# Regrouping the attention stage's PSUM products, its per-engine order and the code bias in a fused embed, attention and ranked-FFN kernel

## The reference, cut to what matters

```
h = h + attn(layernorm(h))      # 12 heads of 64; softmax over the 93 tokens of a sequence
h = h + ffn(layernorm(h))

attn: w = x @ w_qkv
      norm2 = sum over tokens of w*w                  # one per head and channel
      logits = sum over channels of w*w/norm2, * temp
      Pi = softmax(logits);  Pi_norm = Pi / (sum(Pi) + 1e-8)
      dots = sum over tokens of Pi_norm * w*w
      out = -(w * Pi) / (1 + dots);  return out @ w_out + b_out
ffn:  z = x @ P;  scores = z . C                      # 8 groups of 64 keys, 16 wide
      top 4 scores of each group -> softmax -> w
      h = gelu(z @ W1[top] + b1);  y = h @ W2[top] + b2
      code = sum over the four of y*w
      return gelu(code @ G1 + g1b) @ G2 + g2b
```

## Time and profile before

| what | us |
|---|---|
| median of 2 runs (1399.41 and 1400.19) | 1399.8 |
| the profiled execution | 1400.24 |
| its span, first to last instruction | 1398.2 |

### The profile page before, as it was taken

One profiled execution on the slowest core, in us unless ns is written; L12 is line 12 of the kernel. 1 busy time (PEld: TensorE's weight loads), 2 busy tenths in 40 slices (PEclk: granted clock), 3 DMA queues, 4 the chain that ended last, 5 costly groups with the idle time before them and its releaser, 6 DMA issues.

```text
span 1398.2 us, 34230 instructions
## 1 busy us (share of the span) xinstructions
PE 1236.3 (88%) x12232; PEld 622.2 (44%) x12232; DVE 1099.5 (79%) x3359; ACT 1093.8 (78%) x2708; POOL 1007.3 (72%) x724
## 2 busy tenths in 40 slices
PE   3943799999999999858999999999999999999995
PEld 3932466666666666623333333333333333333332
DVE  5682488888888888857878888888888888888883
ACT  0244467776777777339999999999999999999994
POOL 7731467657765776527798888888898888879884
PEclk8966899999999999869999999999999999999997
DMA  9564312222222231133313323232413322241410
GB/s 280 160 126 74 56 53 77 67 70 84 85 68 68 75 97 54 51 107 91 71 38 82 74 61 64 56 75 52 96 48 86 65 57 64 57 92 42 89 38 11
DMA packets 95704, 107.05 MB, mean 77 GB/s; under 512 B 12772, under 2 KB 92668, under 8 KB 95254
## 3 DMA queue, kind: packets, MB, share of 16 engines
q1 hardware_dynamic: 91184, 96.00, 26.6%
q10 hardware_dynamic: 2240, 5.08, 2.2%
q0 software_dynamic: 2112, 3.79, 1.0%
HBM read 67.88 MB, written 33.71 MB: 73 GB/s over the span
## 4 chain that ended last, share of the span: by engine, by line
ACT 28%; PE 11%; POOL 7%; DVE 4%; issue 4%; SPq 1%; DMA 0%; POOLq 0%; DVEq 0%; ACTq 0%
ACT ring L1076 18%; ACT arena L1088 9%; POOL arena L828 5%; PE code L1749 5%; PE ring L1736 5%; DVE arena L1484 4%; PE ring L1768 2%; POOL arena L836 1%; POOL arena L834 1%; ACT arena L1084 0%; DMA bias_codes<-arena 0%; ACT arena L1096 0%; SPq L618 0%; PE ring L1759 0%; SPq L623 0%
## 5 line engine op out<-in xcount | busy, mean ns | idle before, releaser
L1484 DVE TENSOR_TENSOR arena<-ring,arena 128x496 f32<-128x496 f32 x1008 | 611.5, 668 | 132.9 <-ACT ring L1076 129.1
L828 POOL TENSOR_TENSOR arena<-arena 128x992 f32<-128x992 f32 x264 | 608.2, 2316 | 114.1 <-ACT arena L1088 103.1
L1076 ACT ACTIVATE ring<-ring 128x496 f32<-128x496 f32 x1008 | 543.8, 689 | 12.0 <-PE ring L1736 11.1
L1736 PE MATMUL ring<-arena,w_stack 99*32 99x496 bf16 x6144 | 428.3, 375 | 25.9 <-DVE arena L1484 20.0
L1749 PE MATMUL code<-arena,w_pad 128*32 128x496 f32 x3072 | 389.0, 580 | 3.7 <-ACT arena L1092 3.3
L1736 PEld LDWEIGHTS ring<-arena,w_stack 99*32 99x32 bf16 x6144 | 159.7, 95 | 414.9 <-DVE arena L1484 253.1
L1088 ACT ACTIVATE arena<-ring 128x992 f32<-128x992 f32 x252 | 282.7, 1122 | 3.5 <-POOL arena L828 2.8
L1578 PE MATMUL ring<-arena 96*128 96x372 f32 x384 | 135.3, 489 | 1.4 <-ACT arena L932 0.9
L1749 PEld LDWEIGHTS code<-arena,w_pad 128*32 128x32 f32 x3072 | 96.6, 110 | 53.4 <-DVE arena L1484 17.8
L764 POOL TENSOR_TENSOR arena<-arena 128x372 f32<-128x372 f32 x96 | 91.9, 986 | 34.5 <-DVE arena L1324 34.5
L1627 PE MATMUL ring<-arena 128*128 128x376 f32 x192 | 78.5, 534 | 24.2 <-DVE arena L1319 16.0
(11 more groups left out here) (144 smaller groups left out, 1434.8 us busy)
## 6 DMA issues: line engine op xcount, KB each, us to landing
arena<-gates SPq DMA_DIRECT2D x48, 496.0 KB, 6.7
gates<-arena SPq DMA_DIRECT2D x16, 744.0 KB, 11.5
arena<-h_scratch SPq DMA_DIRECT2D x32, 279.0 KB
arena<-z_parts SPq DMA_DIRECT2D x144, 62.0 KB, 2.7
h_scratch<-arena SPq DMA_DIRECT2D x16, 279.0 KB
z_parts<-arena SPq DMA_DIRECT2D x48, 93.0 KB, 2.1
arena<-h_scratch SPq DMA_DIRECT2D x12, 372.0 KB
out_h<-arena SPq DMA_DIRECT2D x12, 372.0 KB
```

The source lines that it names most:

```text
L828: p_.tensor_tensor(spaces[quad % SPACES][:, j:j + 2], hid[:, POOL_DUOS.index(duo) % 2], gst[:, block // EB, j:j + 2], ALU.mult).then_inc(s ...
L1076: a_.activation(product, product, ACT.Gelu_apprx_tanh).then_inc(s_hid, 1)
L1484: v_.tensor_tensor(spaces[quad % SPACES][:, j + p], duo_bank(duo, p), gst[:, block // EB, j + p], ALU.mult).then_inc(s_gat, 1)
L1736: mm = t_.matmul(bank[32 * q:32 * q + 32], w1s[:, x + 32 * q:x + 32 * q + 32], zst[:, o, j + p], start=True, stop=True)
```

## The change: what it does

- `spread_pi` and `scores` become four products each on 32 rows of the contraction, one to a bank: `spread_pi` from `pix`, a tile [128, 94] that needs no placing, so `pi_placed`, `pis`, `unitsel` and `pi_scale_placed` go. Five of the six spreads lie side by side in each bank, and `w_pi` waits for the first five together.
- PSUM is shared out anew: `w_product` has banks 0 to 3, spreads and scores too; logits, bias and scales move to bank 6, z to the code bank.
- `head_weights` becomes one instruction. `mean_term` moves from DVE to POOL, as a negation and a product.
- `pass_sp` loads x first; bias and scales are stored a pass later.
- All five orders are rewritten, with one more pass on SP, ACT and PE.
- Stage 3: ACT's `copy_code` goes, DVE adds the bias straight from PSUM after duo 7, POOL only scales. ACT's table for gelu is loaded after the last `top4_exp`.

```diff
 def pass_sp(i):
-    store_codes(u3), store_bias(u3), store_scales(u3), load_x0(n2), store_h1(u1), load_xr(n1), store_gates(u2)
+    load_x0(n2), store_bias(u4), store_scales(u4), store_gates(u3), store_codes(u2), store_h1(u1), load_xr(n1)
...
+p_.tensor_scalar_mul(nm[k], mv[k][:, :, 0], -1.0)             # in POOL's rstd
+def mean_term(k, u): ... p_.tensor_tensor(nb[k], nm[k], rs[k], ALU.mult)
 def pass_pool(i):
+    attended(u1, 2..5), z_rest(u2), shift(u2, 0), shift(u2, 1), z_part3(u2), rstd("A", n2), residual_biased(u0),
+    rstd("G", u1), mean_term("G", u1), w2_pi(u0, 0), mean_term("A", n2), w2_pi(u0, 1..5), shift(u2, 2), attended(u0, 0..1)
...
 def pass_act(i):
+    w_copy(u1, 3..5), z_copy(u3), z_part1(u3), top4_exp(u4), scores_copy(u3, 0..1), z_part2(u3), scores_exp(u3, 0),
+    scores_copy(u3, 2), logits_exp(u1), gates_copy(u4, 2), scores_exp(u3, 1), gates_copy(u3, 0..1), copy_bias(u4),
+    norm("G", u2), copy_xT("A", u0), norm("A", n1), w_copy(u0, 0), copy_scales(u4), w_copy(u0, 1), copy_xT("G", u2),
+    scores_exp(u3, 2), w_copy(u0, 2)
...
 def pass_dve(i):
+    dots_scaled(u1), bn_stats_x0(n2), dots_negated(u1), top4(u3, 2), neg_attn(u1), mark(u3, 2), norms_floored(u0),
+    norms_inverted(u0), top4_shifted(u3), head_weights(u0), raw(u3, 2), top4_summed(u3), bn_aggr("A", n2),
+    scales_made(u3), top8(u2, 0), logits_tempered(u0), top8(u2, 1), top4(u2, 0), logits_max(u0), mark(u2, 0),
+    pi_recip(u0), top4(u2, 1), pi_made(u0), raw(u2, 0), pi_sum(u0), mark(u2, 1), pi_sum_eps(u0), residual(u1, 0),
+    pi_complete(u0), raw(u2, 1), residual(u1, 1), bn_stats_h1(u1), bn_aggr("G", u1), w_pi(u0, 0..4), attn_dots(u0, 0),
+    w_pi(u0, 5), attn_dots(u0, 1..3), top8(u2, 2), attn_dots(u0, 4..5)
...
 def w_product(u, c):
-    if c < 2: wait(pe, s_rsc, CH * (u - 1) + 5 + c)
-    else: wait(pe, s_wsq, CH * u + c - 1)
+    if c == 0: wait(pe, s_rsc, CH * u)
+    if c >= 4: wait(pe, s_wsq, CH * u + c - 3)
...
 def scores(u, s):
-    wait(pe, s_sc, SUB * u + s)
-    t_.matmul(banks[2][0:ST, :], zf[:, ST * s:ST * s + ST], cbd, ...)
+    if s == 0: wait(pe, s_wsq, min(CH * (u + 3), CH * UNITS)); wait(pe, s_rsc, min(CH * (u + 2), CH * UNITS))
+    for j in range(PAIRS):
+        rows = slice(32 * j, 32 * j + 32)
+        last = t_.matmul(ring[0:ST, j, 128 * s:128 * s + 128], zf[rows, ST * s:ST * s + ST], cbd[rows, 128 * j:128 * j + 128], ...)
...
 def spread_pi(u, c):
-    t_.matmul(pair0[:, c % 2, 0:UB * (N + 1)], headsel[:, c], pis.rearrange("p b n -> p (b n)"), ...)
+    if c == 0: pe.wait_ge(s_wsq, CH * (u + 1)); wait(pe, s_sc, SUB * (u - 1))
+    if c == 5: pe.wait_ge(s_rsc, CH * u + 5)
+    x = (N + 1) * (c % 5)
+    for b in range(UB):
+        rows = slice(32 * b, 32 * b + 32)
+        last = t_.matmul(ring[:, b, x:x + N + 1], headsel[rows, c], pix[rows], ...)
...
 def pass_pe(i):
+    out_product(u2, 2), gates_transposed(u3, 0), spread_pi(u1, 0..4), bias(u4), gates_transposed(u3, 1),
+    scales_transposed(u4), transposes("A", u0), spread_pi(u1, 5), w_product(u0, 0..1), transposes("G", u2),
+    w_product(u0, 2..5), z_product(u2), scores(u2, 0..2), logits(u0), out_product(u1, 0), gates_transposed(u3, 2),
+    out_product(u1, 1)
...
-a_.copy(comb, code_bank[:, 0:TN])                             # ACT, copy_code
-p_.tensor_tensor(biased, comb, bias_t, ALU.add)               # POOL
+v_.tensor_tensor(biased, code_bank[:, 0:TN], bias_t, ALU.add) # DVE, behind duo 7
```

More of the change, by code:

```diff
@@ L981, in logits_exp @@
                 a_.activation(pe_, lg, ACT.Exp, bias=nmax, accum_out=psm).then_inc(s_pe, 1)
-            def pi_placed(u):
-                act.wait_ge(s_pi, u + 1)
-                wait(act, s_pb, CH * u)
-                for b in range(UB):
-                    rows = slice(32 * b, 32 * b + 32)
-                    last = a_.copy(pis[rows, b, 0:N], pi[rows])
-                last.then_inc(s_pip, 1)
             def scores_exp(u, s):
@@ L1016, in pass_act @@
+                if has(u4):
+                    copy_bias(u4)
+                if has(u2):
+                    norm("G", u2, h1)
+                if has(u0):
+                    copy_xT("A", u0)
+                if has(n1):
+                    norm("A", n1, x0)
                 if has(u0):
                     w_copy(u0, 0)
+                if has(u4):
+                    copy_scales(u4)
+                if has(u0):
                     w_copy(u0, 1)
                 if has(u2):
-                    scores_copy(u2, 0)
+                    copy_xT("G", u2)
@@ L1051, in pass_act @@
[L1051 to L1062 removed]
+            for i in range(-1, UNITS + 4):
                 pass_act(i)
[L1064 removed]
@@ L1461, in pass_dve @@
                     top8(u2, 0)
+                if has(u0):
+                    logits_tempered(u0)
+                if has(u2):
+                    top8(u2, 1)
                     top4(u2, 0)
+                if has(u0):
+                    logits_max(u0)
+                if has(u2):
                     mark(u2, 0)
-                    top8(u2, 1)
+                if has(u0):
+                    pi_recip(u0)
+                if has(u2):
                     top4(u2, 1)
-                    mark(u2, 1)
-                    raw(u2, 0)
-            for i in range(-1, UNITS + 3):
+                if has(u0):
+                    pi_made(u0)
+                if has(u2):
+                    raw(u2, 0)
+                if has(u0):
+                    pi_sum(u0)
+                if has(u2):
+                    mark(u2, 1)
+                if has(u0):
+                    pi_sum_eps(u0)
+                if has(u1):
+                    residual(u1, 0)
+                if has(u0):
+                    pi_complete(u0)
+                if has(u2):
+                    raw(u2, 1)
+                if has(u1):
+                    residual(u1, 1)
+                    bn_stats_h1(u1)
+                    bn_aggr("G", u1)
+                if has(u0):
+                    w_pi(u0, 0)
+                    w_pi(u0, 1)
+                    w_pi(u0, 2)
+                    w_pi(u0, 3)
+                    w_pi(u0, 4)
+                    attn_dots(u0, 0)
+                    w_pi(u0, 5)
+                    attn_dots(u0, 1)
+                    attn_dots(u0, 2)
+                    attn_dots(u0, 3)
+                if has(u2):
+                    top8(u2, 2)
+                if has(u0):
+                    attn_dots(u0, 4)
+                    attn_dots(u0, 5)
+            for i in range(-2, UNITS + 3):
                 pass_dve(i)
@@ L1502, in tile_dve @@
                         gate_duo(tile, duo)
+                    if not first and duo == COPY_AFTER:
+                        add_bias(tile - 1)
                     if not first:
@@ L1680, in pass_pe @@
                 if has(u2):
-                    scores(u2, 0)
+                    transposes("G", u2)
                 if has(u0):
@@ L1744, in decode @@
                 if quad == 0:
-                    wait(pe, s_comb, tile)
+                    wait(pe, s_ba, tile)
                 block, k = divmod(quad, KH)
```

384 lines of the change are left out of this document (165 added, 219 removed).

## The result

The changed kernel takes 1416.4 us (median of 1414.74 and 1418.05), the kernel before 1399.8: a ratio of 1.0119, 95% interval 1.0101 to 1.0138. It is 1.2% slower, which is less than 2%. The forecast was 1375, the range 1350 to 1402: the time lies outside.

A forecast was written before the change was run, and what follows sets the result against it. Stage 2 was taken as bound by a loop through one shared bank pair, stage 3 by ACT. Savings of 15.5 (loop) + 2 + 1.4 + 2.5 + 2.2 + 1.2 = 24.8 us from 1400.2 gave 1375, range 1350 to 1402.

The forecast's parts named there:

- the moved `bn_stats_x0`: Stage 2, DVE: the step leaves stretch A, -0.88 us a unit, with no wait for x counted.
- Stretch A: Stage 2 loop, DVE from norms_floored to the last w_pi copy: 14.6 us becomes 16.1, plus 0.3 for the stall.
- rival 1: Stage 2: PE's clock falls in each unit, the first w_product slow, loop 28.6 us, total 1397; chance 0.23.
- stretch B: Stage 2 loop, last w_pi copy over w_product to the next norms_floored: 13.5 us becomes 10.7, ACT the slower side.
- the stall in A: norms_floored held by a POOL instruction: -0.69 us a unit as far as avoided, 0.3 added as part may return.
- `mean_term`, one `head_weights` for four and three short added steps cancel: Stretch A: these altered DVE steps offset one another within some tenths of a us.
- In the steady state the order of the stores is worth nothing: Stage 2, steady units: no gain from reordering stores, since DVE showed no wait for x at bn_stats_x0.
- Rival 4: Stage 2: a new wait, on POOL's mean_term and ACT's norm G, holds the loop near 28.1; 1390 to 1430, chance 0.08.
- Rival 2: Stage 2, PE: row groups run one after another, five spreads 4.3 us, loop 31.6, total 1443; chance 0.07.
- Rival 3: Stage 2: the loop shrinks until DVE's own work bounds it at 25.3 us, total 1348; chance 0.22.
- The start: Start of stage 2: loading x first, ahead of waits for bias and scales, -2 us (0 to -4).
- The end: End of stage 2: gelu table, shift and score waits leave, a longer stretch A adds; together -1.4 us (-4 to +3).

The follow-up runs named there:

- e8: The changed kernel with two buffers for x and each x load issued a whole unit before its use: 1398.0 us.
- e12: e8 with five products added on PE in each unit that nobody reads: 1384.6 us.
- e15: e14 with residual_biased and its load put back where the change has them: 1368.9 us.
- e5: The changed kernel with the store of h1 and the load of the residual's x queued behind the load of x: 1427.8 us.
- e9: The changed kernel with bn_stats_x0 moved on DVE behind mark instead of in front of neg_attn, one x buffer: 1398.9 us.
- e14: e11 with one wait added on POOL, so that z_rest starts only after DVE's raw of the unit before: 1374.3 us.
- e11: e12 with residual_biased and its load moved later, end-of-stage-2 memset behind the last bn_aggr, and a bias store ahead of tile 0's second-half loads: 1381.2 us.
- e1: The changed kernel with a second buffer for x, so that x is loaded a unit earlier: 1412.9 us.

## Why the prediction was wrong

The step that failed most is the term for the moved `bn_stats_x0` (third below): its 0.88 us were taken out of A, and its wait for x was put at nothing. The runs showed 3.65 us of waiting there, which reach A by way of `neg_attn` and `attended`: A is 17.9 us on average, and 16.7 with x in time (e8). Besides it, rival 1 (the clock, in stretch B) was given too low a chance, and the stall in A was sized for one step of four.

- **Stretch B** (10.7): the sum was right, 10.74 in e12, but at a full clock only. "Against it: the gaps are cut by short work" failed: in rows of short products on 32 rows, transposes and waits the granted clock fell once or twice a unit. That was rival 1, priced at a loop of 28.6, 1.5 us a unit above the forecast's; measured with x in time it is 13.4 / 15 = 0.9.
- **Stretch A** (16.1, and 0.3 for the stall): 18.1 in the changed kernel. The stall that I knew from line 1350 was priced for `norms_floored` alone. The new order puts three more two-input steps beside POOL: 0.40 for `top4_shifted`, 0.60 for `head_weights`, 0.72 for `raw` over their shortest. "`mean_term`, one `head_weights` for four and three short added steps cancel" missed that the one `head_weights` stood in the same place as the stall. Without `attended` beside them A is 16.7 (e12), and with `z_rest` away as well 16.2 in e15.
- **The moved `bn_stats_x0`** was counted as 0.88 us out of A, and its wait as nothing: "DVE shows no wait for x at `bn_stats_x0` (456.14)". The old queue showed how far that carries:

```profile
450.56 0.27 SPq L569 DMA_DIRECT2D arena<-h_scratch  x1
```

  Before, the step came 5.6 us after the issue; in the changed kernel DVE is ready for it at 454.10, 3.3 us after the issue at 450.82, and the load takes 6.7 to 6.9 us (e5, and 457.75 - 450.82). After:

```profile
450.82 0.24 SPq L566 DMA_DIRECT2D arena<-h_scratch  x1
```

  Behind it stood `neg_attn`, and behind that POOL's longest run. This is the step that failed most: 17.5 us by e9. "In the steady state the order of the stores is worth nothing" was read from a place that the step then left, and the prediction did not name what was queued behind it.
- **Rival 4** was there in small: ACT waits 0.64 us for POOL in front of norm G, and taking it away gave 2 us. That the measured time lies in its 1390 to 1430 is luck: the waits that held the loop were others. **Rival 2** was wrong and rightly low: five spreads take 1.37 us (forecast 1.0 to 1.3). **Rival 3** did not come: DVE has 3.18 us to spare in e12.
- **The start** (-2): +4.1. x of the first units waited too; with x ahead (e8) the first `pi_complete` comes 29.0 us after the memset, as before. **The end** (-1.4): +2.3, the wait of 5.16 us above.
- **Stage 3**: right in kind, too small in size, -8.1 against -5.9. The start gives 1.8 (from the first `hidden` to the first use of the sum 70.3 us before and 68.5 after) of 2.5, the tiles 3.9 (first to last such step 681.4 and 677.5) of 2.2, the end 2.4 (18.1 and 15.7) of 1.2. The start came as forecast, by the wait for the last stores; but the loads that stood in front of those stores now stand in front of the last store of bias codes but one, and the 5.16 us of ACT at the end of stage 2 are the wait for that. In the tiles ACT loses 11 copies of 0.63 and 2.6 us of waiting for POOL, and waits 15.2 us for PE instead of 9.7: 6.9 + 2.6 - 5.5 = 4.0.

The loop of the forecast, 27.1 in a steady unit, was a sum of engine work that three things on its way (the late x, the clock, `z_rest` beside `raw`) made 29.8 (`norms_floored` from 223.27 to 551.26, eleven units). Taken away, a steady unit takes 26.9 in e14 and 27.0 in e15, and those runs end at 1374 and 1369 us. That 1374 is nearly the forecast's 1375 is in part luck: both runs have e11's end of stage 2, worth 7.3 us, which the forecast did not have.

## What to carry to other kernels

A step that waits for a transfer is moved with its wait: take the distance from issue to use before and after, and ask what is queued behind the step on its engine. Where one instruction is seen to be held by another engine, look at every instruction that the new order puts in that place, not at the one that showed it. A rival that a row supports (the clock fell in one gap) deserves a higher chance when the change makes that gap in every unit.

## What the runs showed of the hardware

- DVE steps with both inputs in SBUF, and the `tensor_scalar` of `norms_floored`, wait until POOL's running instruction ends: 1.38 against 0.69 us for the same `raw` (e11, e14), 1.06 against 0.46 for `head_weights` and 0.70 against 0.18 for `norms_floored` (changed kernel, e9). `w_pi`, one of whose inputs is in PSUM, and the reduction `attn_dots` keep 0.53 and 0.54 beside `w2_pi`. The Trainium skill has this rule (SBUF — State Buffer, Who interferes with whom): a DVE instruction with two SBUF inputs and a GpSimd instruction that reads SBUF exclude one another, and the one that starts first keeps the port until it ends. The runs agree, and the rule would have named three of the four steps from the order alone (`norms_floored` has one input).
- The granted clock fell without a long pause of PE: in the changed kernel, after 2.15 busy of 4.5 us, with no gap above 1.55, it was 0.63 for 4.3 us. Five products a unit that nobody reads held it at 1.00 (e12).
- Four row groups do run side by side: 40 records of 94 columns would take 3.2 us one after another at 0.84 ns a column, and take 1.37.
- A load of 279 KB took 6.7 us with nothing in front of it (e5), at most 5.6 in the kernel before, and 12.8 behind stores (e1: issued 437.36, used 450.21).
